# An attention and feed-forward layer: GpSimd makes the exponentials of 128 columns in every second round, and the weighing runs one round later

## The chip, the cores and the metric

The kernel runs on one core of a Trainium2 chip. The metric is the time of one execution on the device, in microseconds (us). The engines are named as the profile names them: PE is the matrix engine (TensorE), PEld its weight loads, ACT is ScalarE, DVE is VectorE, POOL is GpSimd, and SP issues DMAs. PSUM holds what the matrix engine writes; SBUF is the working memory.

## What is computed

`x` has 4096 tokens of 256 features. The layer normalises it, modulates it by a vector, runs attention with 16 heads of 16 features in which queries, keys and values are the same projection, adds the gated result, normalises again, and runs a feed-forward block of 1024 hidden features with weights that are dequantised from integers.

```python
q = jnp.einsum('bnhd,hed->bnhe', xh, Wq)
scores = jnp.einsum('bnhe,bmhe->bhnm', q, q)
scores = scores / NORM
attn = jax.nn.softmax(scores, axis=-1)
res = jnp.einsum('bhnm,bmhe->bnhe', attn, q)
```

All 4096 x 4096 scores of 16 heads need an exponential: 2.1 million per partition.

## The kernel before, in words

A start stage normalises `x`, makes the projections and keeps them in two fp16 parts, so that a score is one fp16 matmul with 64 rows. An upper bound of each score row goes into that matmul as well, so no maximum is taken later. The long middle stage is the attention, with the feed-forward work of the 512 tokens before laid into it. A tail does the last 512 tokens' feed-forward work by itself.

The middle stage knows these units:

- A **pair** is two score tiles of 128 keys x 512 queries (one in each half of the keys), 128x1024 in PSUM and later in the buffer `probs`. A **group** is 64 pairs: 4 heads (`Q_HEADS`) by 16 key steps, for one chunk of 512 queries. There are 8 chunks of 4 groups, so 32 groups and 2048 pairs.
- A **round** is three pairs. There are 683 rounds (`ROUNDS`). PSUM holds six banks for scores, so three pairs, and each round refills them.
- A **unit** of weighing (`weigh`, L846) is 4 matmuls that multiply one 128x512 half of four pairs by the values and add into `ps_sums`. A group has 32 units.

What each engine does in a round `at`:

- PE, in `scores` (L835): six matmuls. The first two pairs wait for the ACT exponential of the round before, which empties their four banks; the third pair waits for the DVE copy. Then, by the tables of `units` and `places`, one or two units of weighing, and in rounds with one unit most often one **piece** of the feed-forward work of the chunk before (`out_piece`: turning, projecting, `up` and `down`, L854).
- ACT: one exponential over the first two pairs, 128x2048, from PSUM to `probs` (L799, below: the long exponential); in 56 rounds a tanh of 128x512 for the feed-forward work (L793); then one exponential over the third pair, 128x1024, in place in `probs` (L804, the short exponential).
- DVE: `copy_scores` (L1020) copies the third pair, 128x1024, from PSUM to `probs`, and with that frees its two banks; then what the pieces and the norms need (`take_up` L1109, `finish_hidden` L1113, `norms`, `base_of` and others).
- POOL has nothing to do after the start stage.
- SP loads keys and queries, which are read again for every group.

`probs` is a ring of 12 pairs (`P_RING`), four rounds; the engine that fills a place waits (`place_free`) until the weighing has read it (`steps_done`). The order of the work on each engine is fixed in the code; the engines meet through semaphores: `scores_ready`, `copied`, `exps_done`, `steps_done`. Each group ends with the copy and turning of its sums (L991, L860) and a division (`divide`). After the last round the tail turns the attention output, weighs the units that are left, and goes through projection, norms and feed-forward work.

## Time and profile before

| | us |
|---|---|
| median of 3 runs | 2025.85 (2025.77 to 2027.32) |
| the profiled execution, its span | 2023.6 |
| first long exponential starts | 80.90 |
| last long exponential starts | 1966.72 |
| PE busy | 1897.8 (94%) |
| ACT busy | 1938.3 (96%) |
| DVE busy | 1193.2 (59%) |
| POOL busy | 1.3 (0%) |

The profiled execution has no time of its own in the list of runs; its span of 2023.6 us lies 2.25 us under their median. Busy is the time from an instruction's start to its end; ends of matmuls are modelled, and two instructions of one engine can overlap, so the mean times count on the sum more than they do in the span. A start-to-start distance has no such overlap. The idle time beside a group is that of its engine just before its instructions, with what ended it. The granted PE clock is 1.00 of full speed, the level of 2.4 GHz, in the stretches read below.

### The profile page before, as it was taken

The numbers are of one execution on the slowest core, as the hardware profiler recorded it, in microseconds if no ns is written. First come the engines' busy times: TensorE is split into PE (matmuls) and PEld (weight loads), VectorE is DVE, ScalarE is ACT, GpSimd is POOL, SyncE is SP. The second block draws the span as 40 slices with busy tenths as digits, with TensorE's granted clock in tenths as the row PEclk, the third lists the DMA queues.
The fourth block names the chain that finished last, engine by engine and source line by source line (L and its number), as shares of the span: only waits on it lengthen the run. The fifth ranks groups of instructions, "written<-read, shape, count | busy, mean of one in ns | idle before, by whom it ended". The sixth has DMA issues, their size and how long they took to land.

```text
span 2023.6 us, 43276 instructions
## 1 busy us (share of the span) xinstructions
PE 1897.8 (94%) x18477; PEld 550.9 (27%) x18477; DVE 1193.2 (59%) x1632; ACT 1938.3 (96%) x1491; POOL 1.3 (0%) x6
## 2 busy tenths in 40 slices
PE   6888889999999999999999999999999999999998
PEld 5411112222222222222222222222222222222225
DVE  7446455765576555755557555765557555575545
ACT  3899999999999999999999999999999999999992
POOL 0000000000000000000000000000000000000000
PEclk9999999999999999999999999999999999999999
DMA  5541111121212212111111211111121111111100
GB/s 164 144 136 43 40 51 42 48 56 42 52 42 52 52 44 60 46 43 46 52 52 46 58 42 50 44 52 53 43 62 44 40 51 55 49 35 38 42 12 12
DMA packets 121346, 108.14 MB, mean 53 GB/s; under 512 B 21936, under 2 KB 120112, under 8 KB 120896
## 3 DMA queue, kind: packets, MB, share of 16 engines
q1 hardware_dynamic: 120400, 103.69, 19.2%
q8 instruction: 146, 2.39, 0.5%
q10 hardware_dynamic: 752, 1.67, 0.2%
q14 instruction: 48, 0.39, 0.1%
HBM read 96.49 MB, written 8.65 MB: 52 GB/s over the span
## 4 chain that ended last, share of the span: by engine, by line
ACT 78%; issue 11%; PE 6%; DVE 1%; DVEq 0%
ACT attend_probs L799 42%; ACT attend_probs L804 34%; PE attend_sums L846 2%; ACT attend_half_tanh L793 1%; PE attend_scores L835 1%; PE attend_out L854 1%; PE attend_scores L854 1%; DVE attend_probs L1020 0%; DVE attend_st L1038 0%; DVE attend_x L1014 0%; ACT attend_ffn_in L810 0%; PE attend_scores L860 0%; DVE attend_st L1219 0%; DVE z L1230 0%; DVE attend_rs L155 0%
## 5 line engine op out<-in xcount | busy, mean ns | idle before, releaser
L799 ACT ACTIVATE attend_probs<-attend_scores 128x2048 f32<-128x2048 f32 x683 | 1322.1, 1936 | 3.4 <-PE attend_scores L835 3.2
L1020 DVE COPY attend_probs<-attend_scores 128x1024 f32<-128x1024 f32 x682 | 835.1, 1225 | 701.4 <-PE attend_scores L835 692.8
L846 PE MATMUL attend_sums<-attend_probs,values 128*17 128x512 f32 x8192 | 1006.8, 597 | 0.3
L804 ACT ACTIVATE attend_probs<-attend_probs 128x1024 f32<-128x1024 f32 x682 | 762.6, 1118 | 1.2 <-DVE attend_probs L1020 1.2
L835 PE MATMUL attend_scores<-asks,keys 64*128 64x512 f16 x4096 | 562.0, 380 | 99.9 <-ACT attend_probs L799 73.6
L835 PEld LDWEIGHTS attend_scores<-asks,keys 64*128 64x128 f16 x4096 | 149.6, 94 | 711.7 <-ACT attend_probs L799 588.2
L846 PEld LDWEIGHTS attend_sums<-attend_probs,values 128*17 128x17 f32 x8192 | 174.0, 96 | 510.3 <-issue 459.1
L854 PE MATMUL attend_out<-w,hidden 128*32 128x256 f32 x1920 | 124.2, 379 | 0.0
L854 PE MATMUL attend_out<-attend_ffn_in,w 128*32 128x512 f32 x896 | 116.6, 592 | 0.0
L854 PEld LDWEIGHTS attend_out<-w,hidden 128*32 128x32 f32 x1920 | 62.0, 110 | 86.4 <-issue 64.3
L1109 DVE TENSOR_SCALAR attend_half_in<-attend_out,b_col 128x512 f32<-128x512 f32 x56 | 42.1, 751 | 16.3 <-PE attend_out L854 14.8
L854 PEld LDWEIGHTS attend_out<-attend_ffn_in,w 128*32 128x32 f32 x896 | 28.8, 110 | 64.2 <-issue 64.2
L1113 DVE SCALAR_TENSOR_TENSOR hidden<-attend_half_tanh,attend_half_in 128x512 f32<-128x512 f32 x56 | 38.2, 682 | 0.0
L793 ACT ACTIVATE attend_half_tanh<-attend_half_in 128x512 f32<-128x512 f32 x56 | 36.6, 653 | 0.0
L860 PE MATMUL attend_sums<-ident,attend_sums_sb 128*32 128x128 f32 x1024 | 34.6, 276 | 0.6
L991 DVE COPY attend_sums_sb<-attend_sums 128x512 f32<-128x512 f32 x32 | 22.1, 692 | 22.0 <-PE attend_sums L846 22.0
L403 ACT ACTIVATE start_h_feat<-start_ps,mod_col 128x512 f32<-128x512 f32 x16 | 11.5, 774 | 21.8 <-PE start_ps L451 21.8
L854 PE MATMUL attend_out<-wp,attend_att_feat 128*32 128x256 f32 x480 | 31.4, 379 | 0.0
L860 PEld LDWEIGHTS attend_sums<-ident,attend_sums_sb 128*32 128x32 f32 x1024 | 26.1, 109 | 14.9 <-DVE attend_sums_sb L991 14.8
L810 ACT ACTIVATE attend_ffn_in<-attend_scores,beta_col,gamma_col 128x256 f32<-128x256 f32 x4 | 2.0, 560 | 27.7 <-PE attend_scores L854 27.7
L854 PEld LDWEIGHTS attend_out<-wp,attend_att_feat 128*32 128x32 f32 x480 | 15.6, 110 | 22.6 <-issue 17.1
L556 DVE SCALAR_TENSOR_TENSOR start_q_parts<-start_ps,gains,start_q_parts 128x1024 f16<-128x1024 f32 x8 | 10.3, 1283 | 14.9 <-ACT start_q_parts L414 14.8
(146 smaller groups left out, 538.2 us busy)
## 6 DMA issues: line engine op xcount, KB each, us to landing
keys<-parts_dram SPq DMA_DIRECT2D x768, 64.0 KB
keys<-parts_dram SPq DMA_DIRECT2D x256, 56.0 KB
asks<-parts_dram SPq DMA_DIRECT2D x192, 64.0 KB
start_x_in<-L_attn_x SPq DMA_DIRECT2D x8, 512.0 KB, 9.6
parts_dram<-start_q_parts SPq DMA_DIRECT2D x16, 256.0 KB, 2.6
attend_x_now<-L_attn_x SPq DMA_DIRECT2D x8, 512.0 KB, 4.3
out<-base SPq DMA_DIRECT2D x16, 256.0 KB, 2.6
asks<-parts_dram SPq DMA_DIRECT2D x64, 56.0 KB
```

Source lines behind the costliest of these rows:

```text
L403: last = act.activation(h_feat[:, g % 2, k, :], ps_turn[:, k, :], ACT.Identity, bias=mod_col[:, k:k + 1], scale=mod_col[:, 2 + k:3 + k])
L793: act.activation(half_tanh[:, f % 2, :], half_in[:, f % 2, :], ACT.Tanh).then_inc(tanh_done, 1)
L799: act.activation(place(n, 2), ps_scores[:, 0:4, :], ACT.Exp, scale=scale).then_inc(exps_done, 1)
L804: act.activation(place(n + 2), place(n + 2), ACT.Exp, scale=scale).then_inc(exps_done, 1)
L835: last = pe.matmul(ps_scores[:, 2 * i + b, :], keys[rows, part % K_RING, hq, col:col + P], asks[rows, group * Q_HEADS + hq, :], start=True ...
L846: last = pe.matmul(ps_sums[32 * hq:32 * hq + E1, :], values[:, j + STEPS * b, (gg % Q_GROUPS) * Q_HEADS + hq, :], place(gg * PAIRS + Q_HEA ...
L854: last = pe.matmul(to[32 * q:32 * q + 32, :], held[:, 32 * q:32 * q + 32], moved, start=start, stop=stop)
L860: last = pe.matmul(bank[32 * q:32 * q + 32, t * P:(t + 1) * P], source(t)[:, 32 * q:32 * q + 32], ident[:, :], start=True, stop=True)
L991: dve.tensor_copy(sums_sb, ps_sums).then_inc(sums_copied, 1)
L1020: dve.tensor_copy(place(n), ps_scores[:, 4:6, :]).then_inc(copied, 1)
L1109: dve.tensor_scalar(half_in[:, f % 2, :], ps_out, b1_col[:, f:f + 1], 0.5, ALU.add, ALU.mult).then_inc(half_ready, 1)
L1113: dve.scalar_tensor_tensor(out=hidden[:, f, :], in0=half_tanh[:, f % 2, :], scalar=1.0, in1=half_in[:, f % 2, :], op0=ALU.add, op1=ALU.mul ...
```

## The change

In 292 of the 683 rounds the last 128 of the third pair's 1024 columns are no longer exponentiated by ACT. These are the even rounds, without those that meet the rounds 7 to 20 of a chunk's first group (`has_spare`), where DVE works on the norms of the chunk before. DVE scales these columns by the score factor times log2(e) and bounds them below, straight from PSUM into `probs` (`spare_in`), and then copies the other 896. POOL takes two to the power of each by eleven instructions: it rounds to the whole part, subtracts it, evaluates a polynomial of fourth degree as a product of two quadratics in the fraction, builds the power of the whole part from integer bits, and multiplies (`spare_done`). ACT's short exponential covers 896 columns in these rounds. The weighing waits for `spare_done` as well where its four pairs hold new spare columns.

`BEHIND = 1` puts the scores and the DVE copy one round ahead of everything else on PE and DVE; ACT's tanh moves by the same round. `probs` holds 15 pairs instead of 12. The room for it and for POOL's four 128x128 buffers comes from `ffn_in`, which now shares the memory of `att_feat`. One DVE instruction in the start stage makes the factor `exp2_scale`.

```diff
-S_RING, P_RING, K_RING = 3, 12, 4
+S_RING, P_RING, K_RING = 3, 15, 4
+BEHIND = 1
...
+SPARE = 128
+DIRECT = 2 * BANK - SPARE
...
+def has_spare(at):
+    gg = max(g for g in range(GROUPS) if FIRST[g] <= max(at - BEHIND, 0))
+    c, group = divmod(gg, Q_GROUPS)
+    r = at - BEHIND - FIRST[gg]
+    return at % 2 == 0 and at + 1 < ROUNDS and not (c > 0 and group == 0 and 7 <= r <= 20)
...
+                dve.tensor_scalar(exp2_scale, exp_scale, LOG2E, None, ALU.mult).then_inc(gains_ready, 1)
...
-        ffn_in = a.take("ffn_in", DC * BANK).rearrange("p (k n) -> p k n", k=DC)
+        ffn_in = att_feat
+        spare = a.take("spare", 4 * SPARE).rearrange("p (s n) -> p s n", s=4)
...
+            @block.gpsimd
+            def _(pool):
+                whole, part, first, second = (spare[:, i, :] for i in range(4))
+                for k, at in enumerate(SPARE_ROUNDS):
+                    cols = flat(S_RING * at + 2, DIRECT, 2 * BANK)
+                    wait(pool, spare_done, k)
+                    pool.wait_ge(spare_in, k + 1)
+                    pool.tensor_scalar(whole, cols, 1.0, ROUNDER, ALU.mult, ALU.add).then_inc(spare_step, 1)
+                    pool.wait_ge(spare_step, 6 * k + 1)
+                    pool.tensor_scalar(whole, whole, -ROUNDER, 1.0, ALU.add, ALU.mult).then_inc(spare_step, 1)
+                    pool.wait_ge(spare_step, 6 * k + 2)
+                    pool.tensor_tensor(part, cols, whole, ALU.subtract).then_inc(spare_step, 1)
+                    pool.wait_ge(spare_step, 6 * k + 3)
+                    pool.tensor_tensor(cols, part, part, ALU.mult)
+                    pool.tensor_scalar(first, part, CURVE[0][0], CURVE[0][1], ALU.mult, ALU.add)
+                    pool.tensor_scalar(second, part, CURVE[1][0], CURVE[1][1], ALU.mult, ALU.add)
+                    pool.tensor_scalar(whole.bitcast(I32), whole, 2.0 ** 23, LEAD_BITS, ALU.mult, ALU.add).then_inc(spare_step, 1)
+                    pool.wait_ge(spare_step, 6 * k + 4)
+                    pool.tensor_tensor(first, first, cols, ALU.add)
+                    pool.tensor_tensor(second, second, cols, ALU.add).then_inc(spare_step, 1)
+                    pool.wait_ge(spare_step, 6 * k + 5)
+                    pool.tensor_tensor(first, first, second, ALU.mult).then_inc(spare_step, 1)
+                    pool.wait_ge(spare_step, 6 * k + 6)
+                    pool.tensor_tensor(cols, first, whole, ALU.mult).then_inc(spare_done, 1)
...
-                    if at in TANH_IN:
-                        tanh(*TANH_IN[at])
+                    if at - BEHIND in TANH_IN:
+                        tanh(*TANH_IN[at - BEHIND])
                     if at + 1 < ROUNDS:
                         act.wait_ge(copied, at + 1)
-                        act.activation(place(n + 2), place(n + 2), ACT.Exp, scale=scale).then_inc(exps_done, 1)
+                        cols = flat(n + 2, 0, DIRECT if at in SPARE_ROUNDS else 2 * BANK)
+                        act.activation(cols, cols, ACT.Exp, scale=scale).then_inc(exps_done, 1)
...
-                        pe.wait_ge(exps_done, exps_with(gg * PAIRS + Q_HEADS * j + Q_HEADS - 1))
+                        last_pair = gg * PAIRS + Q_HEADS * j + Q_HEADS - 1
+                        pe.wait_ge(exps_done, exps_with(last_pair))
+                        if spares_to(last_pair) > spares_to(last_pair - Q_HEADS):
+                            pe.wait_ge(spare_done, spares_to(last_pair))
...
+                for at in range(BEHIND):
+                    scores_of(at)
                 for gg in range(GROUPS):
                     for r, (begin, end) in enumerate(units(gg)):
                         at = FIRST[gg] + r
-                        for n in range(S_RING * at, min(S_RING * at + S_RING, GROUPS * PAIRS)):
-                            scores(n)
+                        scores_of(at + BEHIND)
...
+                    if at in SPARE_ROUNDS:
+                        dve.tensor_scalar(flat(n, DIRECT, 2 * BANK), bank[:, DIRECT:2 * BANK], exp2_scale, LOWEST,
+                                          ALU.mult, ALU.max).then_inc(spare_in, 1)
+                        dve.tensor_copy(flat(n, 0, DIRECT), bank[:, 0:DIRECT]).then_inc(copied, 1)
+                    else:
+                        dve.tensor_copy(flat(n, 0, 2 * BANK), bank).then_inc(copied, 1)
...
-                        if at + 1 < ROUNDS:
-                            copy_scores(S_RING * at + 2)
+                        copy_scores(at + BEHIND)
```

Three places show what the tables and loops make of it. The first is PE at the end of the middle stage. `attend_scores<-asks,keys` are scores, `attend_sums<-attend_probs,values` is the weighing (x8 is two units), and `attend_scores<-ident,attend_att` begins the tail. Before:

```order
L846 MATMUL attend_sums<-attend_probs,values 17x512 x7
L835 MATMUL attend_scores<-asks,keys 128x512 [waits exps_done]
L835 MATMUL attend_scores<-asks,keys 128x512
L835 MATMUL attend_scores<-asks,keys 128x512 [waits exps_done]
L835 MATMUL attend_scores<-asks,keys 128x512
L846 MATMUL attend_sums<-attend_probs,values 17x512 [waits exps_done]
L846 MATMUL attend_sums<-attend_probs,values 17x512 x7
L860 MATMUL attend_scores<-ident,attend_att 32x128 [waits group_done,copied]
```

And with the change:

```order
L916 MATMUL attend_out<-w,hidden 32x256 x8
L894 MATMUL attend_scores<-asks,keys 128x512 [waits exps_done]
L894 MATMUL attend_scores<-asks,keys 128x512
L894 MATMUL attend_scores<-asks,keys 128x512 [waits exps_done]
L894 MATMUL attend_scores<-asks,keys 128x512
L908 MATMUL attend_sums<-attend_probs,values 17x512 [waits spare_done,exps_done]
L908 MATMUL attend_sums<-attend_probs,values 17x512 x7
L908 MATMUL attend_sums<-attend_probs,values 17x512 [waits spare_done,exps_done]
L908 MATMUL attend_sums<-attend_probs,values 17x512 x7
L922 MATMUL attend_scores<-ident,attend_att 32x128 [waits group_done,copied]
```

Four units of weighing stand behind the last scores where two stood, and they wait for `spare_done`.

The second place is DVE in rounds of the feed-forward `up` pieces. Before:

```order
L1020 COPY attend_probs<-attend_scores 128x1024 [waits steps_done,scores_ready] x2
L1113 SCALAR_TENSOR_TENSOR hidden<-attend_half_tanh,attend_half_in 128x512 [waits tanh_done]
L1109 TENSOR_SCALAR attend_half_in<-attend_out,b_col 128x512 [waits up_mm]
L1020 COPY attend_probs<-attend_scores 128x1024 [waits steps_done,scores_ready] x2
L1113 SCALAR_TENSOR_TENSOR hidden<-attend_half_tanh,attend_half_in 128x512 [waits tanh_done]
```

And with the change:

```order
L1092 TENSOR_SCALAR attend_probs<-attend_scores,gains 128x128 [waits steps_done,scores_ready]
L1094 COPY attend_probs<-attend_scores 128x896
L1096 COPY attend_probs<-attend_scores 128x1024 [waits steps_done,scores_ready]
L1189 SCALAR_TENSOR_TENSOR hidden<-attend_half_tanh,attend_half_in 128x512 [waits tanh_done]
L1185 TENSOR_SCALAR attend_half_in<-attend_out,b_col 128x512 [waits up_mm]
L1092 TENSOR_SCALAR attend_probs<-attend_scores,gains 128x128 [waits steps_done,scores_ready]
L1094 COPY attend_probs<-attend_scores 128x896
```

One copy of two has become two instructions, the 128 columns first; what stands between is in the same order.

The third place is POOL, which has this for each of the 292 rounds:

```order
L825 TENSOR_SCALAR attend_spare<-attend_probs 128x128 [waits spare_in,spare_done]
L827 TENSOR_SCALAR attend_spare<-attend_spare 128x128 [waits spare_step]
L829 TENSOR_TENSOR attend_spare<-attend_probs,attend_spare 128x128 [waits spare_step]
L831 TENSOR_TENSOR attend_probs<-attend_spare 128x128 [waits spare_step]
L832 TENSOR_SCALAR attend_spare<-attend_spare 128x128
L833 TENSOR_SCALAR attend_spare<-attend_spare 128x128
L834 TENSOR_SCALAR attend_spare<-attend_spare 128x128
L836 TENSOR_TENSOR attend_spare<-attend_spare,attend_probs 128x128 [waits spare_step]
L837 TENSOR_TENSOR attend_spare<-attend_spare,attend_probs 128x128
L839 TENSOR_TENSOR attend_spare<-attend_spare 128x128 [waits spare_step]
L841 TENSOR_TENSOR attend_probs<-attend_spare 128x128 [waits spare_step]
```

Five instructions have one tensor as input and six have two; before there was nothing here.

## Rows read from the trace of the kernel before

**Rows 1.** The page: busy time by engine, and the chain that ended last.

```profile
PE 1897.8 (94%) x18477; PEld 550.9 (27%) x18477; DVE 1193.2 (59%) x1632; ACT 1938.3 (96%) x1491; POOL 1.3 (0%) x6
...
ACT 78%; issue 11%; PE 6%; DVE 1%; DVEq 0%
```

**Rows 2.** Windows, two stretches of the middle: length, busy by engine, clock, DMA share, GB/s.

```profile
core 0: us, PE busy (x) PEld busy (x) DVE busy (x) ACT busy (x) POOL busy (x), PEclk, DMA share, GB/s
900.00:1100.00 200.00, 191.78 (x1939) 53.11 (x1934) 120.07 (x155) 199.60 (x150) 0.00 (x0) 1.00 0.21 53
1100.00:1300.00 200.00, 194.57 (x1904) 52.46 (x1896) 114.09 (x123) 200.00 (x153) 0.00 (x0) 1.00 0.18 48
```

**Rows 3.** Groups by line, ACT: count | busy us, mean ns | idle before.

```profile
L799 ACT ACTIVATE attend_probs<-attend_scores 128x2048 f32<-128x2048 f32 x683 | 1322.1, 1936 | 3.4 <-PE attend_scores L835 3.2
L804 ACT ACTIVATE attend_probs<-attend_probs 128x1024 f32<-128x1024 f32 x682 | 762.6, 1118 | 1.2 <-DVE attend_probs L1020 1.2
L793 ACT ACTIVATE attend_half_tanh<-attend_half_in 128x512 f32<-128x512 f32 x56 | 36.6, 653 | 0.0
```

**Rows 4.** Timeline, two plain rounds: start us, us, engine, line, operation.

```profile
1002.14 1.14 ACT L804 ACTIVATE attend_probs<-attend_probs 128x1024 f32<-128x1024 f32 x1
1002.40 0.82 PE L835 MATMUL attend_scores<-asks,keys 64*128 64x512 f16 x6
1003.09 1.96 ACT L799 ACTIVATE attend_probs<-attend_scores 128x2048 f32<-128x2048 f32 x1
1003.26 1.23 DVE L1020 COPY attend_probs<-attend_scores 128x1024 f32<-128x1024 f32 x1 [1.49 <-PE attend_scores L835]
1004.85 1.15 ACT L804 ACTIVATE attend_probs<-attend_probs 128x1024 f32<-128x1024 f32 x1
1005.11 0.82 PE L835 MATMUL attend_scores<-asks,keys 64*128 64x512 f16 x6
1005.79 1.97 ACT L799 ACTIVATE attend_probs<-attend_scores 128x2048 f32<-128x2048 f32 x1
```

**Rows 5.** Timeline, two rounds of `up` with a piece in each.

```profile
639.20 0.82 PE L835 MATMUL attend_scores<-asks,keys 64*128 64x512 f16 x6
639.85 1.88 ACT L799 ACTIVATE attend_probs<-attend_scores 128x2048 f32<-128x2048 f32 x1
641.79 0.82 PE L835 MATMUL attend_scores<-asks,keys 64*128 64x512 f16 x6
642.57 1.87 ACT L799 ACTIVATE attend_probs<-attend_scores 128x2048 f32<-128x2048 f32 x1
644.27 1.04 PE L854 MATMUL attend_out<-attend_ffn_in,w 128*32 128x512 f32 x8
644.32 0.63 ACT L793 ACTIVATE attend_half_tanh<-attend_half_in 128x512 f32<-128x512 f32 x1
644.84 1.05 ACT L804 ACTIVATE attend_probs<-attend_probs 128x1024 f32<-128x1024 f32 x1
645.25 0.82 PE L835 MATMUL attend_scores<-asks,keys 64*128 64x512 f16 x6
```

**Rows 6.** Groups by line, DVE.

```profile
L1020 DVE COPY attend_probs<-attend_scores 128x1024 f32<-128x1024 f32 x682 | 835.1, 1225 | 701.4 <-PE attend_scores L835 692.8 <-issue 1.3
L1109 DVE TENSOR_SCALAR attend_half_in<-attend_out,b_col 128x512 f32<-128x512 f32 x56 | 42.1, 751 | 16.3 <-PE attend_out L854 14.8
L991 DVE COPY attend_sums_sb<-attend_sums 128x512 f32<-128x512 f32 x32 | 22.1, 692 | 22.0 <-PE attend_sums L846 22.0
```

**Rows 7.** Groups by line, POOL.

```profile
L388 POOL MEMSET values<- 128x512 f32 x1 | 1.0, 1001 | 0.0
L387 POOL MEMSET start_ones<- 128x128 f32 x1 | 0.2, 205 | 0.3 <-POOLq L1283 0.3
L1283 POOL MEMSET const-float32-1.0<- 128x1 f32 x1 | 0.1, 99 | 0.0
```

**Rows 8.** Timeline, DVE: two instructions of which the second waits for the first.

```profile
1979.09 0.17 DVE L138 TENSOR_SCALAR attend_rsqrt_work<-attend_mo 128x2 f32<-128x2 f32 x1
1979.30 0.17 DVE L140 TENSOR_SCALAR attend_rsqrt_work<-attend_rsqrt_work 128x2 int32<-128x2 int32 x1
```

**Rows 9.** Timeline, the last round and the start of the tail.

```profile
1966.59 1.91 PE L846 MATMUL attend_sums<-attend_probs,values 128*17 128x512 f32 x16
1966.72 1.99 ACT L799 ACTIVATE attend_probs<-attend_scores 128x2048 f32<-128x2048 f32 x1
1968.31 1.06 PE L860 MATMUL attend_scores<-ident,attend_att 128*32 128x128 f32 x32
1969.19 1.04 PE L846 MATMUL attend_sums<-attend_probs,values 128*17 128x512 f32 x8
```

**Rows 10.** Timeline, ACT: the first long exponential.

```profile
80.90 1.88 ACT L799 ACTIVATE attend_probs<-attend_scores 128x2048 f32<-128x2048 f32 x1 [1.70 <-PE attend_scores L835]
```

More of the change, by code:

```diff
@@ L97, with spares_to @@
 PIECE_IN, TANH_IN, HIDDEN_IN = plan()
+SPARE = 128
+DIRECT = 2 * BANK - SPARE
+LOG2E = 1.4426950408889634
+LOWEST = -118.0
+ROUNDER = 1.5 * 2.0 ** 23
+CURVE = ((0.7988556027412415, 13.09467887878418), (5.044106960296631, 7.979714870452881))
+LEAD_BITS = float((127 - 7) * 2 ** 23 + 1887232)
+def has_spare(at):
[3 more added lines that the diff above has]
+    return at % 2 == 0 and at + 1 < ROUNDS and not (c > 0 and group == 0 and 7 <= r <= 20)
+SPARE_ROUNDS = [at for at in range(ROUNDS) if has_spare(at)]
+def spares_to(n):
+    return sum(S_RING * at + 2 <= n for at in SPARE_ROUNDS)
 def exps_with(n):
@@ L725, in place, with flat @@
             return probs[:, first:first + 2 * pairs, :]
+        def flat(n, lo, hi):
+            first = 2 * (n % P_RING)
+            return probs[:, first:first + 2, :].rearrange("p s n -> p (s n)")[:, lo:hi]
         def place_free(eng, n):
@@ L929, in out_piece, with scores_of @@
                             down(t, f, ps_out[:, (t % 2) * D:(t % 2 + 1) * D])
+                def scores_of(at):
+                    for n in range(S_RING * at, min(S_RING * at + S_RING, GROUPS * PAIRS)):
+                        scores(n)
+                for at in range(BEHIND):
+                    scores_of(at)
                 for gg in range(GROUPS):
@@ L1015, in residual, with copy_scores @@
                                       x_now[:, 2 * b:2 * b + 2, :], ALU.add).then_inc(x1_ready, 1)
-                def copy_scores(n):
+                def copy_scores(at):
+                    if at + 1 >= ROUNDS:
+                        return
+                    n = S_RING * at + 2
+                    bank = ps_scores[:, 4:6, :].rearrange("p s n -> p (s n)")
                     dve.wait_ge(scores_ready, n + 1)
                     place_free(dve, n)
-                    dve.tensor_copy(place(n), ps_scores[:, 4:6, :]).then_inc(copied, 1)
+                    if at in SPARE_ROUNDS:
[4 more added lines that the diff above has]
+                        dve.tensor_copy(flat(n, 0, 2 * BANK), bank).then_inc(copied, 1)
                 def add_bias(o):
@@ L1179, in weights @@
                             dve.tensor_tensor(w2[:, k, :], w2[:, k, :], sign[:, 0, :], ALU.mult).then_inc(w_step, 1)
+                for at in range(BEHIND):
+                    copy_scores(at)
                 for gg in range(GROUPS):
```

8 lines of the change are left out of this document (4 added, 4 removed).

## The prediction

> **What bounds the kernel now.** I read the page first: ACT is busy 96% of the span, PE 94%, DVE 59%, and 78% of the chain that ended last is ACT [rows 1]. Two shares near the top don't say which engine holds the other up, so the windows come next: in the middle, ACT is busy 199.6 and 200.0 us of 200, PE 192 and 195, POOL nothing, and the PE clock is at its full level [rows 2]. The groups by line settle it. The 683 long exponentials have 3.4 us of idle time before them in all, and the 682 short ones 1.2 us [rows 3]: ACT goes from one straight to the next, and who else waits, waits for ACT.
>
> A timeline of two plain rounds gives the period [rows 4]. Long to short exponential, start to start, is 1.76 us (1003.09 to 1004.85), short to long 0.95 (1002.14 to 1003.09), together 2.70 or 2.71. Beside it runs a second loop, which the reader should see, because it limits what a shorter ACT round can give: the long exponential empties the banks, 0.06 us after its end PE starts the next scores (5.11), and 0.68 to 0.69 us after that the next long exponential starts (2.40 to 3.09). With 1.96 us for the exponential itself that is 2.70 us, no less than ACT's own period. But its length isn't fixed. Where ACT had to wait before it, it takes 1.87 to 1.88 us and starts 0.65 us after the scores [rows 5]; back to back with a short one it takes up to 1.99 [rows 9]. The mean is 1.94 [rows 3]. So part of the 1.96 is time in which the instruction before still runs, and the loop by itself needs 1.88 + 0.06 + 0.65 = 2.59 us.
>
> One stretch is PE's. Where a feed-forward piece stands in every round, two rounds take 6.05 us (639.20 to 645.25), and the one with three blocks of work takes 3.46 us from scores to scores [rows 5]: the piece there starts at 644.27, the scores at 645.25, with nothing between. By the plan's tables there are 66 rounds whose piece follows a piece in the round before, in the second group of seven chunks.
>
> **The change, part by part.**
>
> ACT's saving. 128 columns leave the short exponential. The price of a column: a tanh of 512 holds ACT 0.52 us (644.32 to 644.84) [rows 5], an exponential of 1024 0.95 [rows 4], so 0.43/512 = 0.84 ns a column and 0.107 us for 128. From the long and the short one, (1.76 - 0.95)/1024 = 0.79 ns, so 0.101. From mean lengths, (1118 - 653)/512 = 0.91 ns [rows 3], so 0.116. I take 0.105; the ends are 0.101 and 0.116. The round then asks for 2.71 - 0.105 = 2.605 us, just above the loop's 2.59. PE by itself needs 3.46 less one block of about 0.86 (two of weighing lie between 642.54 and 644.27 in its round), so 2.60. Both fit, by 5 to 15 ns.
>
> How often. 292 rounds are spared. In the 66 rounds of the PE-bound stretches, 33 of them spared, a shorter exponential ends no sooner what PE ends late, so they give nothing. 259 x 0.105 = 27.2 us.
>
> DVE. Its instruction of 128 columns out of PSUM with a column of scalars doesn't occur. The same form with 512 takes 751 ns, and a copied column (1225 - 692)/512 = 1.04 ns [rows 6]; so 751 - 384 x 1.04 = 352 ns, and the copy of 896 columns 1092. Together 1.44 us for 1.23. Now the copy ends at 1004.49, and the short exponential starts at 1004.85 [rows 4]: of 0.36 us in hand 0.14 are left. Cost nothing, with that cover; each later 0.1 us would take back all of what a spared round gives.
>
> POOL. Eleven instructions in a row per spared round, with a new set every second round, so they have 2.605 + 2.71 = 5.3 us. The trace has no such instruction. The nearest row is a memset of the same 128x128 tile, 205 ns [rows 7]. From below: 11 x 0.205 + 6 hand-overs x 0.04 (as on DVE, 1979.09 + 0.17 to 1979.30 [rows 8]) = 2.5 us. From above: the strided memset costs (1001 - 99)/512 = 1.76 ns a column [rows 7], with its start-up 0.325 us for 128; at twice that for two inputs, and hand-overs as long as a one-element memset, 5 x 0.325 + 6 x 0.65 + 6 x 0.1 = 6.1. I take the tile's own row, doubled for two inputs, with 0.1 for a hand-over: 5 x 0.205 + 6 x 0.41 + 6 x 0.1 = 4.1 us. That is nearest in shape and stride, and it fits in 5.3. The first weighing that reads spare columns stands three rounds behind their scores, which is about 8.0 + 0.75 - 0.86 - 0.35 = 7.5 us after they are in memory, so a set of 4.1 is in time, and PE's new wait finds its semaphore set. [...]
>
> The round's delay. Each pair is weighed one round later and the ring is three pairs longer, so who waits for a free place waits no longer. In the middle it costs nothing. At the end PE has two more units behind the last scores; two take 1.72 us (1966.59 to 1968.31), and the tail's leftover weighing at 1969.19 comes after the exponential's end at 1968.71, so PE holds it [rows 9]. Add 1.7. The added DVE instruction at the start is another 0.17 us like those of [rows 8], at most 0.2.
>
> **Sum.** -27.2 + 1.7 + 0.2 = -25.3 us, all between the first exponential at 80.90 [rows 10] and the tail. The profiled span of 2023.6 becomes 1998.3; the runs stand 2.25 above that span, so **2000.5 us**, 1.25% under 2025.85.
>
> **Rivals.**
>
> 1. *The loop of scores keeps most of it.* If the long exponential stays at 1.96 us in spared rounds, the loop needs 1.96 + 0.06 + 0.65 = 2.67, and a spared round saves 0.04: 259 x 0.04 = 10.4 us, less 1.9 at both ends, **2017.3**. For it: the sums fit by only 5 to 15 ns, and a round that starts a new part of the keys has one wait more on PE. Against it: every exponential that had to wait in [rows 5] is short.
>
> 2. *POOL is the bound (the other side).* At 5.9 us a set, not quite my upper end, 292 sets are 1723 us; the 98 rounds without spare work add 98 x 2.705 = 265, the stretches at 6.05 another 5, and some 11 come back where the queue empties before seven such gaps. That makes 1982 for what takes 1885.8 now (80.90 to 1966.72 [rows 9, 10]): +96, with the tail **2124**. It decides from about 5.6 us a set; at 5.3 it costs nothing. In the trace PE would stand at the weighing, for `spare_done`. For it: six of the instructions have two inputs, one writes integers, six wait for the one before. Against: my estimate leaves a quarter free.
>
> 3. *DVE comes late through POOL.* If a copy has to wait while a POOL instruction of 0.2 to 0.4 us runs, it ends 0.2 us past what the short exponential can bear: 259 x 0.2 = 52 us lost against 27 gained, **2053**. Against it: DVE reads PSUM here, and is idle 41% of the span [rows 1]. The page SBUF — State Buffer of the Trainium skill (section Who interferes with whom) says that DVE and GpSimd share a pair of ports and block each other for a whole instruction, but only where DVE has two inputs in SBUF or runs in a two-port mode; by that rule the copies are free, and only the 56 `finish_hidden` and some sums are held up, in rounds with time to spare.
>
> 4. *It cancels out.* A set of about 5.6 us, or copies 0.1 us too late: **2025**.
>
> **How the numbers follow.** My forecast 0.64, rival 1 0.16, rival 2 0.12, rival 3 0.04, rival 4 0.04. The low end takes the dearest column in all spared rounds, 292 x 0.116 = 33.9, less 1.9: 1993.9, so 1993. The high end takes in rival 1: 2018. That holds 0.80. A difference of 0.2%, 4 us, is about what a measurement of this kernel can tell from none. Faster: forecast and rival 1, 0.80. Within 0.2%: 0.04. Slower: rivals 2 and 3, 0.16.
>
> **What would show it.** Short exponentials of 896 columns with 0.84 us to the next long one; long ones in spared rounds near 1.88 us, and the two periods 2.60 and 2.71; DVE's pair near 1.44 us with no idle ACT time behind it; a POOL set near 4.1 us, so POOL about 65% busy in the middle; PE not waiting for POOL. Wrong it would be with idle time before long exponentials released by the scores (rival 1), PE released by POOL at the weighing (rival 2), or idle time before short ones released by DVE (rival 3).

## The result, and the profile after

The changed kernel takes **2002.08 us** (median of 4 runs, 2001.95 to 2002.4) against 2026.2 for the kernel before on the same chip (2025.77 to 2027.32): ratio 0.9881, 95% interval 0.9867 to 0.9895. The forecast was 2000.5. The profiled execution has a span of 2000.0 us.

The page of the changed kernel, busy time and chain (for [rows 1]):

```profile
PE 1884.5 (94%) x18477; PEld 549.5 (27%) x18477; DVE 1239.2 (62%) x1925; ACT 1907.8 (95%) x1491; POOL 1269.7 (63%) x3218
...
ACT 69%; PE 16%; issue 9%; DVE 2%; ACTq 0%; DVEq 0%
```

ACT still leads the chain, but PE's part has gone from 6% to 16%: with a shorter ACT round, more of the time is PE's. POOL is 63% busy over the span and 68% between the first and the last long exponential (1268 of 1861 us). The forecast of about 65% came near by luck: its own sets, with 3.5 us of work each, would make 292 x 3.5 us, 55%; the sets measured have 4.3 us of work.

Groups by line, shapes apart, ACT and DVE (for [rows 3, 6]):

```profile
L857 ACT ACTIVATE attend_probs<-attend_scores 128x2048 f32<-128x2048 f32 x683 | 1294.8, 1896 | 7.8 <-PE attend_scores L894 4.7
L863 ACT ACTIVATE attend_probs<-attend_probs 128x1024 f32<-128x1024 f32 x390 | 419.2, 1075 | 1.9 <-DVE attend_probs L1096 1.9
L863 ACT ACTIVATE attend_probs<-attend_probs 128x896 f32<-128x896 f32 x292 | 283.0, 969 | 0.0
...
L1094 DVE COPY attend_probs<-attend_scores 128x896 f32<-128x896 f32 x292 | 315.5, 1081 | 0.0
L1092 DVE TENSOR_SCALAR attend_probs<-attend_scores,gains 128x128 f32<-128x128 f32 x292 | 102.4, 351 | 266.2 <-PE attend_scores L894 263.9
```

The reader should see three things. The short exponential of 896 columns is 106 ns shorter than the one of 1024, and never waits. The long one has fallen from 1936 to 1896 ns with 7.8 us of idle time before all 683 (3.4 before). DVE's pair is 0.351 + 1.081 us.

Timeline of the changed kernel, a spared and a plain round, ACT, PE's scores, and the set on POOL (for [rows 4]):

```profile
1001.83 1.90 ACT L857 ACTIVATE attend_probs<-attend_scores 128x2048 f32<-128x2048 f32 x1
...
1002.45 0.30 POOL L825 TENSOR_SCALAR attend_spare<-attend_probs 128x128 f32<-128x128 f32 x1 [0.40 <-DVE attend_probs L1092]
...
1003.21 0.46 POOL L829 TENSOR_TENSOR attend_spare<-attend_probs,attend_spare 128x128 f32<-128x128 f32 x1
1003.59 0.97 ACT L863 ACTIVATE attend_probs<-attend_probs 128x896 f32<-128x896 f32 x1
1003.75 0.40 POOL L831 TENSOR_TENSOR attend_probs<-attend_spare 128x128 f32<-128x128 f32 x1
1003.78 0.82 PE L894 MATMUL attend_scores<-asks,keys 64*128 64x512 f16 x6
...
1004.43 1.90 ACT L857 ACTIVATE attend_probs<-attend_scores 128x2048 f32<-128x2048 f32 x1
...
1006.20 1.07 ACT L863 ACTIVATE attend_probs<-attend_probs 128x1024 f32<-128x1024 f32 x1
...
1006.83 0.46 POOL L841 TENSOR_TENSOR attend_probs<-attend_spare 128x128 f32<-128x128 f32 x1
...
1007.15 1.89 ACT L857 ACTIVATE attend_probs<-attend_scores 128x2048 f32<-128x2048 f32 x1
```

The spared round lasts 2.60 us (1001.83 to 1004.43), with 0.84 from the short to the next long exponential; the plain one 2.72 (to 1007.15). POOL's set runs from 1002.45 to 1007.29, 4.84 us, and the next begins 0.47 us later, when DVE has the new columns ready.

The end of the middle stage (for [rows 9, 10]), with the first long exponential ahead of it:

```profile
80.94 1.88 ACT L857 ACTIVATE attend_probs<-attend_scores 128x2048 f32<-128x2048 f32 x1 [1.79 <-PE attend_scores L894]
...
1941.28 3.63 PE L908 MATMUL attend_sums<-attend_probs,values 128*17 128x512 f32 x32
1941.51 1.89 ACT L857 ACTIVATE attend_probs<-attend_scores 128x2048 f32<-128x2048 f32 x1
1944.72 1.05 PE L922 MATMUL attend_scores<-ident,attend_att 128*32 128x128 f32 x32
1945.60 1.90 PE L908 MATMUL attend_sums<-attend_probs,values 128*17 128x512 f32 x16
```

From the first to the last long exponential it is 1860.57 us, where it was 1885.82: **-25.25**. From there to the end of the span it is 58.49, where it was 56.88: **+1.61**. The start is 0.04 later. That is the whole difference of the spans, -23.60.

### The profile page after: what moved, and what is told of

It reads as the page before. It is cut to its first block, busy times and chain, and to the rows that moved or that the text cites. A ratio compares the mean times of both kernels' runs of the same rounds, so it can differ in the third digit from the quotient of the medians.

```text
span 2000.0 us, 47347 instructions
## 1 busy us (share of the span) xinstructions
PE 1884.5 (94%) x18477; PEld 549.5 (27%) x18477; DVE 1239.2 (62%) x1925; ACT 1907.8 (95%) x1491; POOL 1269.7 (63%) x3218
## 4 chain that ended last, share of the span: by engine, by line
ACT 69%; PE 16%; issue 9%; DVE 2%; ACTq 0%; DVEq 0%
ACT attend_probs L857 40%; ACT attend_probs L863 29%; PE attend_sums L908 7%; PE attend_scores L894 4%; PE attend_out L916 3%; PE attend_scores L916 1%; ACT attend_half_tanh L851 1%; DVE attend_probs L1096 0%; PE attend_out L922 0%; PE attend_sums L922 0%; DVE w L1255 0%; DVE attend_st L1114 0%; DVE attend_x L1081 0%; ACT attend_att_feat L869 0%; PE attend_scores L922 0%
## 5 line engine op out<-in xcount | busy, mean ns | idle before, releaser
L857 ACT ACTIVATE attend_probs<-attend_scores 128x2048 f32<-128x2048 f32 x683 | 1294.8, 1896 | 7.8 <-PE attend_scores L894 4.7
L1096 DVE COPY attend_probs<-attend_scores 128x1024 f32<-128x1024 f32 x390 | 477.4, 1224 | 372.4 <-PE attend_scores L894 367.7
L863 ACT ACTIVATE attend_probs<-attend_probs 128x1024 f32<-128x1024 f32 (+1 forms) x682 | 702.2, 1030 | 1.9 <-DVE attend_probs L1096 1.9
L1094 DVE COPY attend_probs<-attend_scores 128x896 f32<-128x896 f32 x292 | 315.5, 1081 | 0.0
L1092 DVE TENSOR_SCALAR attend_probs<-attend_scores,gains 128x128 f32<-128x128 f32 x292 | 102.4, 351 | 266.2 <-PE attend_scores L894 263.9
L829 POOL TENSOR_TENSOR attend_spare<-attend_probs,attend_spare 128x128 f32<-128x128 f32 x292 | 147.9, 506 | 24.3
L839 POOL TENSOR_TENSOR attend_spare<-attend_spare 128x128 f32<-128x128 f32 x292 | 147.4, 505 | 22.9
L841 POOL TENSOR_TENSOR attend_probs<-attend_spare 128x128 f32<-128x128 f32 x292 | 141.4, 484 | 22.9
L836 POOL TENSOR_TENSOR attend_spare<-attend_spare,attend_probs 128x128 f32<-128x128 f32 x292 | 139.0, 476 | 24.3
L837 POOL TENSOR_TENSOR attend_spare<-attend_spare,attend_probs 128x128 f32<-128x128 f32 x292 | 137.6, 471 | 0.0
L831 POOL TENSOR_TENSOR attend_probs<-attend_spare 128x128 f32<-128x128 f32 x292 | 117.5, 403 | 22.9
L916 PE MATMUL attend_out<-attend_att_feat,w 128*32 128x512 f32 x896 | 116.6, 592 | 0.0
L827 POOL TENSOR_SCALAR attend_spare<-attend_spare 128x128 f32<-128x128 f32 x292 | 89.3, 306 | 24.1
L832 POOL TENSOR_SCALAR attend_spare<-attend_spare 128x128 f32<-128x128 f32 x292 | 89.4, 306 | 19.7
L833 POOL TENSOR_SCALAR attend_spare<-attend_spare 128x128 f32<-128x128 f32 x292 | 88.7, 304 | 18.2
```

What stands on the lines that cost most here:

```text
L829: pool.tensor_tensor(part, cols, whole, ALU.subtract).then_inc(spare_step, 1)
L836: pool.tensor_tensor(first, first, cols, ALU.add)
L837: pool.tensor_tensor(second, second, cols, ALU.add).then_inc(spare_step, 1)
L839: pool.tensor_tensor(first, first, second, ALU.mult).then_inc(spare_step, 1)
L841: pool.tensor_tensor(cols, first, whole, ALU.mult).then_inc(spare_done, 1)
L857: act.activation(place(n, 2), ps_scores[:, 0:4, :], ACT.Exp, scale=scale).then_inc(exps_done, 1)
```

## The experiments

Ratios are against runs of the kernel before on the same chip. Experiments 1 to 4 share such runs; so do 5 to 7 with the second kernel of 8, and the first kernel of 8 with 9.

**1. The delay alone.** No round is spared and POOL has no work; the ring of 15 pairs and `BEHIND = 1` stay.

```diff
-SPARE_ROUNDS = [at for at in range(ROUNDS) if has_spare(at)]
+SPARE_ROUNDS = []
```

> No column is spared: ACT makes all exponentials again, POOL does nothing, DVE copies all 1024 columns; the round's delay, the ring of 15 pairs and the start's extra instruction stay. Theory (ACT is the bound, the delay only costs at the ends): the kernel before plus 1.6 us at the tail and up to 0.9 us in the first rounds, so 2027.5 to 2029 us, with plain rounds back at 2.70 to 2.72. Rival (part of the gain is the delay's, because PE and DVE work is freed from waits): below 2022 us.

2027.25 us, ratio 1.0011 (1.0002 to 1.0021). From the first to the last long exponential it takes 1885.82 us, as before; behind that 58.57, so +1.69. The equal middle is a balance: the first group is 0.50 us longer, where PE's clock was longer at its low level than before (see ACT's saving, below), and the other thirty-one together are 0.50 shorter. So the delay by itself gives half a microsecond in the middle at most, and costs the tail's 1.7.

**2. The spared columns without the delay.**

```diff
-BEHIND = 1
+BEHIND = 0
```

> The spared columns without the round's delay (BEHIND = 0, ring of 15 kept). In the changed kernel POOL ends a set 6.2 us after PE began that round's scores; without the delay most sets (203 of 292) are read by the weighing two rounds on, about 2.60 + 2.71 + 0.75 = 6.07 us after. Theory: PE then waits some 0.2 us for POOL at each of these, two rounds take about 5.5 us, and the kernel comes to 2030 to 2040 us, no faster than before. Rival (the delay is not needed): about 2000 us, the tail's 1.6 us less.

2042.87 us, ratio 1.0086 (1.0069 to 1.0103), a little above what was expected. PE's waits in this kernel (us in total, times, longest):

```profile
PE attend_sums L908 <- POOL attend_probs L841: 45.1, 87, 3.0
```

These are fewer and longer waits than expected (some 200 of 0.2 us). The changed kernel has one such wait, of 1.2 us. So the delay is what gives POOL's set its time: for 1.7 us it saves some 40.

**3. No work on POOL.** All else is as in the change; the weighing waits for DVE's columns (`spare_in`), which go into it without their exponential.

```diff
-                            pe.wait_ge(spare_done, spares_to(last_pair))
+                            pe.wait_ge(spare_in, spares_to(last_pair))
```

> POOL's eleven instructions are left out; the spared 128 columns stay without an exponential, and the weighing waits for DVE's scaled columns instead. Theory (POOL's work is hidden, apart from the stretch where DVE prepares the weights): 2000.5 to 2002 us. Rival (POOL and DVE block each other over the whole run, or PE waits for POOL): 1990 us or less.

1999.84 us, ratio 0.9874 (0.9858 to 0.9891). First to last long exponential: 1859.14 us, 1.43 less than with POOL. Compared group by group, from the starts of the long exponentials, 0.42 of it lies in the first group and 0.90 in the second; in each of the other thirty it is 0.01 or less. The first group's 0.42 is less than two executions of the same work differ by there (see ACT's saving, below), so it isn't shown to be POOL's. POOL's 1270 us of work are hidden but for the second group.

**4. One more instruction a set**, a two-input one on the same columns whose result nobody reads.

```diff
+                    pool.tensor_tensor(extra, part, part, ALU.mult)
```

> One more POOL instruction with two inputs in each set, its result unused. Undisturbed sets follow each other 4.93 us apart where POOL is behind; this makes them about 5.35 us, against 5.32 us for two rounds. Theory (POOL has about 0.4 us in hand per two rounds): 2002 to 2011 us, PE released by POOL at some weighings. Rival (POOL is hidden with room to spare, because the weighing stands three rounds behind): 2002 us and no wait for POOL.

2012.26 us, ratio 0.9939 (0.9923 to 0.9956): just above the upper end of what was expected. PE's waits:

```profile
PE attend_sums L909 <- POOL attend_probs L842: 12.6, 17, 2.9
```

0.33 us more a set (5.17 in the median) cost 12 us. POOL had little in hand.

**5. All 341 even rounds spared**, with those where DVE does the norms.

```diff
-    return at % 2 == 0 and at + 1 < ROUNDS and not (c > 0 and group == 0 and 7 <= r <= 20)
+    return at % 2 == 0 and at + 1 < ROUNDS
```

> The 49 second rounds that the change leaves alone, where VectorE normalizes and prepares, are spared too: 341 in all. Theory A (each spared round outside the stretches that TensorE bounds gives 0.105 us, and VectorE's work there leaves room): 49 x 0.105 = 5.1 us less, 1997. Theory B (VectorE's two-input work there and GpSimd's sets lengthen each other, as at 170.76 us of the changed kernel, and TensorE or ScalarE waits for it): nothing gained or some lost, 2002 to 2010.

2009.29 us, ratio 0.9923 (0.9906 to 0.9939): 49 more spared rounds made it slower. Timeline of this kernel, DVE and ACT in `modulate`, between the copies of two rounds:

```profile
356.13 1.28 DVE L1136 SCALAR_TENSOR_TENSOR attend_hid<-attend_x,attend_mo,mod 128x256 f32<-128x256 f32 x2
...
358.28 1.21 DVE L1096 COPY attend_probs<-attend_scores 128x1024 f32<-128x1024 f32 x1
...
359.53 1.06 ACT L863 ACTIVATE attend_probs<-attend_probs 128x1024 f32<-128x1024 f32 x1 [0.54 <-DVE attend_probs L1096]
```

And the changed kernel at the same place, where POOL has no set:

```profile
358.25 0.87 DVE L1136 SCALAR_TENSOR_TENSOR attend_hid<-attend_x,attend_mo,mod 128x256 f32<-128x256 f32 x2
...
359.95 1.22 DVE L1096 COPY attend_probs<-attend_scores 128x1024 f32<-128x1024 f32 x1
```

With two inputs in SBUF, DVE's pair goes from 0.87 to 1.28 us beside POOL; the copies out of PSUM stay at 1.21. The copy comes late, and ACT waits. Three such places in each of the seven chunks add 9.2 us to their rounds in all; the other spared rounds there give a part of it back. Theory B holds.

**6. 256 columns off the short exponential, no POOL.**

```diff
-SPARE = 128
+SPARE = 256
```

> 256 instead of 128 columns leave the short exponential of every spared round, and GpSimd makes none of them (they stay without an exponential). Theory A (a spared round already stands at the loop of long exponential, scores and back, 1.89 + 0.055 + 0.65 = 2.597 us, which the short exponential is no part of): the same time as with 128 columns and no GpSimd, 1998 to 2001, with idle time of about 0.1 us before each long exponential of a spared round, put down to TensorE. Theory B (ScalarE's own sum still sets the period): 259 x 0.105 = 27 us less again, 1973.

1994.4 us, ratio 0.9846 (0.983 to 0.9863). Timeline of a spared round of this kernel:

```profile
1003.06 1.87 ACT L836 ACTIVATE attend_probs<-attend_scores 128x2048 f32<-128x2048 f32 x1
...
1004.82 0.84 ACT L842 ACTIVATE attend_probs<-attend_probs 128x768 f32<-128x768 f32 x1
...
1004.99 0.82 PE L873 MATMUL attend_scores<-asks,keys 64*128 64x512 f16 x6
1005.63 1.88 ACT L836 ACTIVATE attend_probs<-attend_scores 128x2048 f32<-128x2048 f32 x1
```

The period is 2.57 us: the exponential's 1.87, 0.06 to the scores, 0.64 from there to the next long exponential. A second 128 columns would be worth another 27 us to ACT alone and gave 5.4. The loop of scores does stop it, as theory A has it, but its length is 2.571, not 2.597, and the time is 4 us under A's range. The sign that A names hardly shows:

```profile
L836 ACT ACTIVATE attend_probs<-attend_scores 128x2048 f32<-128x2048 f32 x683 | 1282.9, 1878 | 10.6 <-PE attend_scores L873 8.9
```

That is 10.6 us of idle time, where 0.1 in each spared round would be 29. The short exponential takes 0.84 us and the next long one starts 0.81 after its start, where 896 columns take 0.97 and the next starts after 0.84: most of what ACT loses to the loop is the overlap of the two. The changed kernel's spared round is still ACT's, with 26 ns in hand.

**7. 128 columns off every round but the normalizing ones, no POOL.**

```diff
-    return at % 2 == 0 and at + 1 < ROUNDS and not (c > 0 and group == 0 and 7 <= r <= 20)
+    return at + 1 < ROUNDS and not (c > 0 and group == 0 and 7 <= r <= 20)
```

> 128 columns leave the short exponential of every round but the normalizing ones, not of every second, and GpSimd makes none of them (they stay without an exponential). Theory A (the rounds that are not spared stand at 2.72 us for ScalarE alone, and the loop's 2.60 is open to them too): the other 259 rounds outside the stretches that TensorE bounds give 0.12 us each, 31 us less than with every second round, about 1969. Theory B (TensorE's own work, 2.60 us a round and more where a piece of the other work stands in it, averages over the two rounds and leaves no room for a second spared one): a part of it alone, 1980 to 1995.

1977.9 us, ratio 0.9766 (0.975 to 0.9782), 21.9 under experiment 3: between the two theories, 9 us over A's time and 2 under B's range. Plain rounds stand at 2.60 to 2.61 us, one after another, so PE sustains them; two rounds with `up` pieces still take 6.05. A round further off ACT is thus worth some 0.09 us; what is missing is an engine that would make these columns.

**8. Ten instructions a set, in the change's rounds and in all even rounds.** Adding the rounding constant and taking it away again become one instruction.

```diff
-                    pool.tensor_scalar(whole, cols, 1.0, ROUNDER, ALU.mult, ALU.add).then_inc(spare_step, 1)
-                    pool.wait_ge(spare_step, 6 * k + 1)
-                    pool.tensor_scalar(whole, whole, -ROUNDER, 1.0, ALU.add, ALU.mult).then_inc(spare_step, 1)
+                    pool.tensor_scalar(whole, cols, ROUNDER, -ROUNDER, ALU.add, ALU.add).then_inc(spare_step, 1)
```

> The same rounds as in the change, 128 columns, but ten instructions a set on GpSimd, some 0.37 us less (4.83 to about 4.46). Theory A (GpSimd's length is hidden but for the two first groups, which cost 1.4 us in all by the run without GpSimd): the same as the changed kernel or at most 1 us less, 2001 to 2002. Theory B (a set costs something in every spared round): 292 x 0.01 us or more, 1999 or less.

> All 341 second rounds are spared, and the set on GpSimd has ten instructions, not eleven: adding the rounding constant and taking it away again is one tensor_scalar with two scalars, so a set is some 0.37 us shorter (4.83 to about 4.46 in an undisturbed one). Theory A (a set that is longer than 4.9 us against VectorE's work is what made TensorE wait in the changed kernel's second group, and the shorter one clears it): 1.5 us less than with all second rounds and eleven instructions, near 1995.5. Theory B (GpSimd's length is wholly hidden, so a shorter set gives nothing): the same as with eleven instructions within 0.5 us.

2000.34 us, ratio 0.9878 (0.9862 to 0.9893), and with all even rounds 2011.54, ratio 0.9931 (0.9914 to 0.9947). The second is 2.3 us over experiment 5, outside both theories; 2.0 of it lies in the first two groups of the seven later chunks, and its cause stays open. Neither set is 0.37 us shorter. POOL's groups in the first of the two kernels:

```profile
L825 POOL TENSOR_SCALAR attend_spare<-attend_probs 128x128 f32<-128x128 f32 x292 | 187.7, 643 | 494.1 <-DVE attend_probs L1090 488.2 <-POOL attend_probs L839 0.3
...
L830 POOL TENSOR_SCALAR attend_spare<-attend_spare 128x128 f32<-128x128 f32 x292 | 88.1, 302 | 19.8
```

The instruction with two additions takes 643 ns, the one with a product and a sum 302. So one of 643 replaces two of 300 and a hand-over of 0.08, and the set falls by 0.06 us, to 4.78. These two runs can't decide what a set 0.37 us shorter would give; a slightly shorter one gives nothing that the times can tell, and clears the wait in the second group.

**9. Other rounds, and more columns.** 314 rounds are spared: of the normalizing groups those whose set doesn't meet `modulate` and what follows, and of the second group none that meets `weights`. Then the same with ten instructions and 144 or 160 columns.

```diff
-    ... and not (c > 0 and group == 0 and 7 <= r <= 20)
+    ... and not (c > 0 and group == 0 and 14 <= r <= 20) and not (gg == 1 and 5 <= r <= 11)
```

> Other rounds are spared, 314 in all: of the normalizing groups those whose set does not run against VectorE's two modulating steps, its second root and its last normalizing (26 more), and of the second group none whose set runs against the preparing of the weights (4 fewer). Theory A (GpSimd and VectorE hold each other up only where VectorE reads two inputs from SBUF): 26 x 0.105 = 2.7 us gained, 0.4 given up, 0.9 of waits gone, so 3.2 us under the changed kernel, 1999. Theory B (any VectorE work in the normalizing groups is lengthened enough to make ScalarE wait): no less than the changed kernel, 2002 or more.

> The 314 rounds of the kernel with other rounds, ten instructions a set, and 144 columns instead of 128. By the run with 256 columns a plain spared round can go from 2.597 to 2.571 us before the loop of scores holds it, and a column is 0.84 ns. Theory A (a set of about 4.46 + 0.3 = 4.75 us still fits): 16 columns give 13 ns in some 315 rounds, 4 us, so 1995. Theory B (the set is too long against VectorE's other work): 2000 or more, with TensorE waiting for GpSimd.

> As with 144 columns, but 160. The loop's end is just reached: 26 ns in some 280 rounds and as much where a tanh stands, 8 us under the kernel with other rounds, 1991, if the set fits. The set would be about 5.05 us; by the run with one more instruction (5.25 us, 12 us lost) it is near the end of what fits. Theory A (5.3 us a set is the limit, and stretches where VectorE lengthens a set are few): 1991 to 1994. Theory B (what the set needs in hand is over 0.25 us, since VectorE lengthens one in most pieces): over 1997, with TensorE waiting for GpSimd ten times or more.

With 128 columns 2000.59 us, ratio 0.9878 (0.9863 to 0.9894); with 144 columns 1999.97, ratio 0.9876 (0.986 to 0.9891); with 160 columns 2034.78, ratio 1.0046 (1.0033 to 1.006). The first two can't be told from the changed kernel by time. With 144 columns the groups where nothing waits give 0.10 to 0.15 us each, as 16 columns should; where PE waits for POOL (2.9 us in eight waits) and in the normalizing groups it is lost again.

The trace says where the first one's 3.2 us went. In the second group 0.46 us are gained, as forecast (0.9 of waits, less 4 x 0.105); 0.32 more lie in the first group, where both kernels have the same work. In four of the seven chunks three or four more spared rounds give 0.32 to 0.35: each gives its 0.105, and where there are four, a later round takes 0.07 back. In the other three chunks four more spared rounds *cost* 0.17 in all: two of the four lose 0.10 to 0.13 each, because there DVE was already late, and a later round loses 0.13. Timeline of this kernel at such a round:

```profile
351.05 1.88 ACT L857 ACTIVATE attend_probs<-attend_scores 128x2048 f32<-128x2048 f32 x1
...
352.21 0.32 DVE L1092 TENSOR_SCALAR attend_probs<-attend_scores,gains 128x128 f32<-128x128 f32 x1
352.45 1.08 DVE L1094 COPY attend_probs<-attend_scores 128x896 f32<-128x896 f32 x1
...
353.56 0.95 ACT L863 ACTIVATE attend_probs<-attend_probs 128x896 f32<-128x896 f32 x1 [0.63 <-DVE attend_probs L1094]
```

And the changed kernel there:

```profile
351.08 1.89 ACT L857 ACTIVATE attend_probs<-attend_scores 128x2048 f32<-128x2048 f32 x1
...
352.14 1.19 DVE L1096 COPY attend_probs<-attend_scores 128x1024 f32<-128x1024 f32 x1
...
353.37 1.06 ACT L863 ACTIVATE attend_probs<-attend_probs 128x1024 f32<-128x1024 f32 x1 [0.40 <-DVE attend_probs L1096]
```

From long to short exponential it is 2.51 us instead of 2.29, since both wait for DVE and DVE's pair is longer than the one copy; ACT gains 0.105, and a loss of 0.10 to 0.13 is left in such a round. Theory A had left this out: not only lengthened instructions count, a round without cover does too.

The kernel with 160 columns is rival 2, made to happen. PE's waits in it, and the place where a set grows:

```profile
PE attend_sums L906 <- POOL attend_probs L839: 39.7, 79, 2.0
```

```profile
291.41 1.39 DVE L1098 TENSOR_TENSOR attend_x_now<-attend_x_now,bp_ga 128x1024 f32<-128x1024 f32 x1
291.80 1.31 POOL L829 TENSOR_TENSOR attend_probs<-attend_spare 128x160 f32<-128x160 f32 x1
...
296.04 0.52 POOL L839 TENSOR_TENSOR attend_probs<-attend_spare 128x160 f32<-128x160 f32 x1
...
296.71 0.62 PE L906 MATMUL attend_sums<-attend_probs,values 128*17 128x512 f32 x4 [1.19 <-POOL attend_probs L839]
```

A POOL instruction of 0.45 us takes 1.31 beside DVE's sum of two SBUF tensors; sets stand back to back (0.09 from the end of one to the next), and PE waits for the last instruction.

Put together, the set's length (median of all sets, first start to last end) against what it costs:

| kernel | set, us | PE waits for POOL, us (times) | ratio |
|---|---|---|---|
| ten instructions | 4.78 | none | 0.9878 |
| the change | 4.84 | 1.2 (1) | 0.9881 |
| ten, 144 columns, 314 rounds | 5.09 | 2.9 (8) | 0.9876 |
| one more instruction | 5.17 | 12.6 (17) | 0.9939 |
| ten, 160 columns, 314 rounds | 5.36 | 39.7 (79) | 1.0046 |

No kernel of these beats the changed one by more than the intervals allow.

## Why the prediction was right, step by step

**ACT's saving.** The mechanism and its size held. 0.84 us from short to long exponential, a period of 2.60, 106 ns between the two forms. The sum of 27.2 us for 259 rounds stands against 26.7 in the run without POOL (1885.82 to 1859.14) and 25.25 in the change. The stretches bound by PE gave nothing, as assumed: two rounds with `up` pieces take 6.05 us in both kernels.

The 1.9 us that are missing lie in the two first groups, which saved 0.07 and 0.25 us where a group with ten or eleven spared rounds, without the stretches bound by PE, saves 1.01 to 1.14. Two causes are seen there. In the second group DVE prepares the weights, and POOL and DVE hold each other up. Timeline of the changed kernel:

```profile
170.38 1.38 DVE L1250 SCALAR_TENSOR_TENSOR w<-w,hidden 128x1024 f32<-128x1024 int32 x1
...
170.76 1.32 POOL L839 TENSOR_TENSOR attend_spare<-attend_spare 128x128 f32<-128x128 f32 x1
...
176.04 2.32 DVE L1255 TENSOR_TENSOR w<-w,z 128x256 f32<-128x256 f32 x4
...
178.22 1.05 PE L908 MATMUL attend_sums<-attend_probs,values 128*17 128x512 f32 x8 [1.21 <-POOL attend_probs L841]
```

Without POOL, DVE's instruction takes 1.22 us; POOL's usually takes 0.46. The one wait of PE for POOL, and the 0.90 us that experiment 3 gets back in this group, come from here; experiment 9, which only leaves four rounds of this group unspared, gets back 0.46 net. That is rival 3's mechanism, by DVE's two-input instructions and not by its copies. The prediction looked for them in `finish_hidden` and some sums, with time to spare, and left out the weights, where there was none. The rule of the Trainium skill that was cited (SBUF — State Buffer, Who interferes with whom) agrees with these rows: the copies out of PSUM are 1.08 us with POOL and without.

In the first group PE's clock counts. Windows of four us, before (length, PE, PEld, DVE, ACT, POOL, clock, DMA share, GB/s):

```profile
88.00:92.00 4.00, 4.00 (x30) 0.58 (x22) 1.26 (x2) 2.65 (x3) 0.00 (x0) 0.77 0.45 115
```

And after:

```profile
88.00:92.00 4.00, 3.52 (x18) 0.78 (x22) 1.55 (x2) 3.75 (x4) 3.41 (x10) 0.50 0.42 123
92.00:96.00 4.00, 3.74 (x22) 0.42 (x14) 1.20 (x2) 1.88 (x2) 0.92 (x3) 0.69 0.44 126
```

With the delay PE has no weighing beside the first scores (1.46 us of work from 84 to 88, for 2.46 before). It stands at 0.50 of full speed, the level of 1.2 GHz, through the window from 88 to 92, where before it had begun to rise. The first double block of weighing takes 3.61 us there. The first five rounds take 16.17 us, for 15.44 before, though three of them are spared. But the same work can go faster: experiment 5's kernel is the same program as the change up to the second chunk, with the same sets on POOL, and its windows (its first long exponential starts 1.2 us earlier) are

```profile
88.00:92.00 4.00, 4.00 (x26) 0.70 (x22) 1.23 (x1) 2.92 (x3) 2.69 (x7) 0.69 0.41 112
92.00:96.00 4.00, 3.22 (x29) 0.80 (x30) 2.54 (x4) 3.99 (x3) 2.73 (x8) 1.00 0.52 140
```

There the double block takes 2.77 us, the first five rounds 14.90, and the first group saves 1.35 us, where the change's saves 0.07. In the other kernels with the delay the five rounds take 14.92 to 16.07 (15.97 in experiment 1, which spares none). So the part of the 1.9 that lies in this group, about 1 us, goes with the clock, which stayed low longer in the change's profiled execution than this work needs, and not with POOL. Whether the delay makes a long low stretch more likely, single executions can't show.

**DVE.** 0.352 and 1.092 were forecast; 0.351 and 1.081 measured. The cover held: nothing waits before the short exponentials of 896 columns. It is larger than forecast: in the spared round shown above DVE's copy ends at 1003.28, 0.31 us before the short exponential, where 0.14 was worked out; the two instructions overlap by 0.08. Experiment 9 shows the price without cover, a net loss of 0.10 to 0.13 in such a round.

**POOL.** The term was mis-sized: 4.1 us forecast, 4.84 measured, inside the bounds of 2.5 to 6.1. POOL's groups of the changed kernel (for [rows 7]):

```profile
L829 POOL TENSOR_TENSOR attend_spare<-attend_probs,attend_spare 128x128 f32<-128x128 f32 x292 | 147.9, 506 | 24.3
...
L834 POOL TENSOR_SCALAR attend_spare<-attend_spare 128x128 int32<-128x128 f32 x292 | 92.4, 316 | 18.2
```

By the timeline an undisturbed instruction takes 0.30 us with one input (0.205 forecast), 0.46 with two (0.41 forecast), and 0.40 with one tensor as both. The memset was too cheap a neighbour; doubling it for two inputs came near. Hand-overs of 0.08 us were forecast as 0.1. So 5 x 0.30 + 0.40 + 5 x 0.46 = 4.20, and the gaps make up the rest of 4.84. "My estimate leaves a quarter free" was wrong: it left 0.37 us of 5.30 with the 0.09 to the next set, a fourteenth.

**The point from which POOL decides.** It was put at about 5.6 us, by setting sets against seven gaps without work. That sum was held against the 1885.8 us of the kernel before; against the change's 1860.6 it gives 5.5. The runs show the first waits in numbers at 5.09 (2.9 us) and a loss clear of the intervals at 5.17. What was missed is that sets are not all alike: 51 of 292 take over 5.3 us, the longest 7.50, each of them beside DVE work with two inputs in SBUF. So the change's mean set is 5.02 us where the median is 4.84; in experiment 4 the mean is 5.37, above the 5.30 of two rounds, and a set of 5.17 with 5.30 to do it in has 0.04 us each time to catch up.

**The delay.** +1.7 forecast, +1.61 measured in the change and +1.69 with the delay alone. PE's new wait found its semaphore set in all rounds but one, and experiment 2 shows that this is the delay's doing.

**Rival 1** fell by the period: 2.60 us in a spared round, not 2.67, with the long exponential at 1.90. Its own sign, idle time before long exponentials, is 7.8 us in all, but that says little, since it is only 10.6 where the loop does stop ACT (experiment 6). The loop by itself is 2.571 us, where 2.59 was worked out, and PE keeps to that too, where 2.60 was worked out for it. The 0.65 us from scores to exponential rests on one row of [rows 5], 639.85: the exponential at 642.57 starts 0.78 after its scores, behind a short one that ends at 642.67, so it had not waited for them. Experiment 6's 0.64 bears the figure out. The loop's 26 ns decide nothing here and end the gain at about 160 columns.

## What to carry to other kernels

When a balanced engine sheds work to an idle one, size the idle engine's chain against the full period, and keep room in the usual length for the sets that other engines stretch: here 0.46 us in 5.3 were enough, though 51 sets outlasted the period, and 0.13 were not. Work moved on behind by one round costs only its units at the end and can be what makes a slow helper free. Before giving more rounds to it, look for the rounds in which a third engine already ends last: there the split itself costs more than the move saves.

## What was not expected of the hardware

- On POOL a TENSOR_SCALAR of 128x128 takes 300 ns with a product and a sum and 643 ns with two additions.
- On POOL a two-input instruction goes from 458 to 527 ns between 128 and 160 columns (medians over the sets of the first kernel of experiment 8 and of the last of experiment 9), 2.15 ns a column; a one-input one from 298 to 324, 0.81 ns. The GPSIMD Engine Reference of the Trainium skill (Elementwise — side-by-side cycle accounting) gives 2.6 cycles at 1.2 GHz for two inputs, which is 2.17 ns and agrees. Its 1.03 cycles for a short body (k up to 2), 0.86 ns, is near the 0.81 measured for one input; its 1.8 cycles, 1.5 ns, the best case of a tight loop, is nearly twice that.
- A POOL instruction of 0.46 us can last 1.32 beside one of DVE with two inputs in SBUF, and DVE's pair of 0.87 goes to 1.28: each holds the other up.
